# Attention scores on 32-row tiles of the array, causal masks off TensorE, a ring of four PSUM banks

## The reference, cut to what matters

```python
def _L0_attn_ref(x, Wq, bq, Wk, bk, Wv, bv, Wo, bo):
    B, T, C = x.shape
    H, D = (N_HEADS, HEAD_DIM)                # 16 heads of 8
    scale = D ** (-0.5)
    q = (x @ Wq + bq).reshape(B, T, H, D).transpose(0, 2, 1, 3)
    ...
    scores = jnp.einsum('bhqd,bhkd->bhqk', q, k) * scale
    pos = (jnp.arange(T)[:, None] - jnp.arange(T)[None, :]).astype(jnp.float32)
    bias = alibi_slopes(H)[:, None, None] * pos
    scores = scores + bias[None]
    causal = jnp.tril(jnp.ones((T, T), dtype=bool))
    scores = jnp.where(causal, scores, -jnp.inf)
    attn = jax.nn.softmax(scores, axis=-1)
    out = jnp.einsum('bhqk,bhkd->bhqd', attn, v)
    out = out.transpose(0, 2, 1, 3).reshape(B, T, C)
    return out @ Wo + bo
...
x = x + _layernorm(_L0_attn_ref(_layernorm(x, axis=-1), ...), axis=-1)
x = x + _layernorm(_L0_ffn_ref(_layernorm(x, axis=-1), ...), axis=-1)
```

## Time and profile before

| what | us |
|---|---|
| median of 3 runs | 2289.69 (2287.66 to 2295.19) |
| span of the profiled execution | 2287.5 |
| lowest run, beside that span | 2287.66 |

### The profile page before, as it was taken

How to read it: one execution, slowest core, us unless ns; L and a number is a source line. 1 busy time by engine, 2 the same in 40 slices (tenths; PEclk the granted TensorE clock), 3 DMA queues, 4 the chain that set the end, 5 groups by cost and what they waited for, 6 DMA issues and landing times. The chain is left out here.

```text
span 2287.5 us, 41083 instructions
## 1 busy us (share of the span) xinstructions
PE 2102.9 (92%) x11100; PEld 1223.1 (53%) x11100; DVE 1671.8 (73%) x3157; ACT 1373.5 (60%) x2647; POOL 977.3 (43%) x744
## 2 busy tenths in 40 slices
PE   5899999999999679999999999999993999999996
PEld 4455555555554534555555555555531666666664
DVE  5766667666672787777777777778822899998986
ACT  4266566666666616666666666666672655555654
POOL 3665464553610355333333333342002466565554
PEclk7799999999999679999999999999996999999998
DMA  2000000000000300000000000000001100000000
GB/s 59 1 2 1 3 1 1 2 2 1 1 1 2 110 0 1 2 1 1 2 1 1 2 1 1 1 1 1 1 1 61 51 19 19 2 19 19 19 10 10
DMA packets 27508, 24.96 MB, mean 11 GB/s; under 512 B 2409, under 2 KB 21110, under 8 KB 27282
## 3 DMA queue, kind: packets, MB, share of 16 engines
q1 hardware_dynamic: 26400, 21.91, 3.2%
q10 hardware_dynamic: 882, 0.36, 0.1%
HBM read 13.87 MB, written 6.29 MB: 9 GB/s over the span
## 5 line engine op out<-in xcount | busy, mean ns | idle before, releaser
L466 DVE TENSOR_REDUCE at_mx<-at_a 128x1 f32<-128x512 f32 (+3 forms) x1632 | 1010.8, 675 | 358.7 <-PE at_a L333 249.5
L415 ACT ACTIVATE at_probs<-at_b 128x512 f32<-128x512 f32 (+3 forms) x1792 | 888.6, 558 | 474.0 <-PE at_b L360 292.7
L333 PE MATMUL at_a<-at_km,at_fq 128*128 128x512 f32 (+1 forms) x1632 | 704.8, 439 | 20.4 <-DVE at_mx L466 9.8
L360 PE MATMUL at_b<-at_fqm,at_km 128*128 128x512 f32 (+3 forms) x1792 | 710.8, 404 | 11.4 <-ACT at_probs L415 7.6
L333 PEld LDWEIGHTS at_a<-at_km,at_fq 128*128 128x128 f32 x1632 | 316.3, 194 | 290.0 <-DVE at_mx L466 224.4
L360 PEld LDWEIGHTS at_b<-at_fqm,at_km 128*128 128x128 f32 x1792 | 339.8, 191 | 205.5 <-ACT at_probs L415 120.3
L378 PE MATMUL at_pv<-at_probs,at_vst 128*32 128x512 f32 (+3 forms) x3584 | 437.9, 561 | 1.5 <-ACT at_probs L415 1.5
L556 POOL TENSOR_TENSOR at_hi<-at_u,split_sign 128x512 fp32r<-128x512 f32 x120 | 124.9, 1041 | 441.1 <-ACT at_u L404 306.5
L1172 ACT ACTIVATE t_hid<-t_bank_h,b1t 128x512 f32<-128x512 f32 x256 | 174.3, 689 | 195.9 <-DVE t_hid_lo L1306 113.1
L1306 DVE TENSOR_TENSOR t_hid_lo<-t_hid,t_hid_hi 128x512 fp32r<-128x512 f32 x256 | 225.6, 917 | 15.0 <-ACT t_hid_hi L1179 11.8
L569 POOL TENSOR_TENSOR at_km<-at_fk,head_mask 128x2048 fp32r<-128x2048 f32 x60 | 216.1, 3602 | 11.2 <-POOL at_fk L567 11.0
(11 more groups left out here) (211 smaller groups left out, 2410.3 us busy)
## 6 DMA issues: line engine op xcount, KB each, us to landing
t_raw<-L_ffn_W SPq DMA_DIRECT2D x16, 256.0 KB, 3.1
x_first<-L_attn_x SPq DMA_DIRECT2D x4, 512.0 KB, 7.3
second_x_in<-L_attn_x SPq DMA_DIRECT2D x8, 256.0 KB, 3.1
kept<-second_joined SPq DMA_DIRECT2D x8, 256.0 KB, 2.6
kept_u<-second_normed SPq DMA_DIRECT2D x8, 256.0 KB, 2.0
t_heads_in<-tokens SPq DMA_DIRECT2D x8, 256.0 KB, 2.6
t_u_in<-kept_u SPq DMA_DIRECT2D x8, 256.0 KB, 3.1
t_x_in<-kept SPq DMA_DIRECT2D x8, 256.0 KB, 3.1
```

What stands on the lines that cost most here:

```text
L333: mm = pe.matmul(scores, fq[g][:, qt * P:(qt + 1) * P], km[g][:, heads[0]:heads[0] + k, kh * HALF:kh * HALF + w], start=True, stop=not dia ...
L360: mm = pe.matmul(out[:, 0:w], km[g][:, j, kt * P:(kt + 1) * P], fqm[g % 2][:, q0:q0 + w], start=True, stop=not diagonal)
L415: act.activation(probs[(t % 2) * GH + j][:, 0:w], b_bank[n % 3][:, 0:w], ACT.Exp).then_inc(exp_done, 1)
L466: dve.tensor_reduce(mx[:, kh, qt, heads[0]:heads[0] + k], a_bank[n % 3][:, 0:k * w].rearrange("p (k w) -> p k w", k=k), AX.X, ALU.max).the ...
```

## The change

1. Score matmuls contract over 32 partitions, those of their head, for both "a" and "b". The array's other rows stay free for the neighbour in the queue. `km` and `head_mask` go, and with them one instruction of four in the split of keys; `fk` takes the split keys directly.
2. The four "b" of a quad run over the heads 2, 3, 0, 1, so that "a" of head 0, 1, 2, 3 between them lie on other rows.
3. No mask matmuls. An "a" chunk that ends on the diagonal is read by `tensor_tensor_reduce`, which adds a row of zeros and mask and takes the maximum in one pass; chunks are no longer joined over heads (48 in a causal round, 32 of them "ragged", 8 each of 128, 256, 384 and 512 columns; 64 as before in the other attention). For "b" the exponentials of a diagonal quad are taken without a mask and GpSimd's `affine_select` puts zeros over them before "pv", eight quads a round.
4. "a", proj, otr and mtr share one ring of four PSUM banks in the order of the list. "b" keeps three.
5. "b" is three quads ahead instead of two, "pv" trails it by two steps instead of one, and `probs` holds four quads.

```diff
+RING = ("a", "proj", "otr", "mtr")
+A_BANKS = 4
+B_BANKS = 3
+PROBS = 4
...
-                per = max(1, HALF // n)
-                per = 4 if per >= 4 else per
-                for j in range(0, GH, per):
-                    self.chunks.append((qt, kh, list(range(j, j + per)), n))
+                for j in range(GH):
+                    self.chunks.append((qt, kh, j, n))
...
-        self.lead = 2
-        a_steps = nq - 4
+        self.lead = 3
+        a_steps = nq - 2 - self.lead
...
-            dp, p = (ds, q - 1) if q else (0, self.nq - 1)
+            dp, p = (0, i + 1) if i + 1 < self.nq else (1, 0)
...
+def b_head(n):
+    return (n + 2) % GH
...
+                        rows = slice(HW * j, HW * (j + 1))
+                        mm = pe.matmul(misc[:, 0:w], fq[g][rows, qt * P:(qt + 1) * P],
+                                       fk[g][rows, kh * HALF:kh * HALF + w],
+                                       start=True, stop=True)
...
+                        out = b_bank[n % B_BANKS]
+                        rows = slice(HW * j, HW * (j + 1))
+                        mm = pe.matmul(out[:, 0:w], fk[g][rows, kt * P:(kt + 1) * P],
+                                       fqm[g % 2][rows, q0:q0 + w], start=True, stop=True)
...
+                        if n in plan.diagonals:
+                            done(pe, masked, len(plan.diagonals), s, plan.diagonals.index(n))
...
+                        if n in plan.ragged:
+                            ragged = plan.ragged.index(n)
+                            if ragged >= 2:
+                                done(dve, a_read, NA, s, plan.ragged[ragged - 2])
+                            dve.sem_inc(dve_passed, 1)
+                            dve.tensor_tensor_reduce(scrap[ragged % 2][:, 0:w], scores, causal_rows[:, HALF - w:HALF], 1.0,
+                                                     -3.0e38, ALU.add, ALU.max,
+                                                     mx[:, kh, qt, j:j + 1]).then_inc(a_read, 1)
+                        else:
+                            dve.tensor_reduce(mx[:, kh, qt, j:j + 1], scores, AX.X, ALU.max).then_inc(a_read, 1)
...
+                    if what == "b" and n % GH == GH - 1 and n // GH in plan.diagonals:
+                        await_(exp_done, NB, s, n)
+                        block_ = probs[n // GH % PROBS][:, :, 0:P]
+                        pool.affine_select(block_, block_, [[0, GH], [1, P]], ALU.is_ge, 0.0, base=0,
+                                           channel_multiplier=-1).then_inc(masked, 1)
```

More of the change, by code:

```diff
@@ L67, in __init__ @@
                     continue
-                per = max(1, HALF // n)
-                per = 4 if per >= 4 else per
-                for j in range(0, GH, per):
-                    self.chunks.append((qt, kh, list(range(j, j + per)), n))
+                for j in range(GH):
+                    self.chunks.append((qt, kh, j, n))
+        self.ragged = [i for i, (qt, kh, j, n) in enumerate(self.chunks) if causal and kh * HALF + n == (qt + 1) * P]
         self.quads = []
@@ L76, in __init__ @@
                 self.quads.append((qh, kt))
+        self.diagonals = [t for t, (qh, kt) in enumerate(self.quads) if causal and kt * P >= qh * HALF]
         self.na = len(self.chunks)
@@ L135, in body, with places @@
         return out
+    def places(self, steps):
+        order = [step for step in steps if step[0] in RING]
+        return {step: place for place, step in enumerate(order)}
     def prologue(self):
@@ L387, in emit @@
                         mm.then_inc(o_turned, 1)
+                if prologue:
+                    done(pe, proj_read, 4, s0 + 2, 3)
+                    done(pe, fqm_made, 2, s0, 1)
+                    done(pe, a_read, NA, s0 + 1, plan.a_next - 1)
             run(pe, emit)
@@ L458, in emit @@
+                        dve.tensor_tensor(dst[g][:, half], part[:, :], un[:, :], ALU.add).then_inc(split_done, 1)
                     elif what == "a":
-                        qt, kh, heads, w = plan.chunks[n]
+                        qt, kh, j, w = plan.chunks[n]
                         done(dve, a_made, NA, s, n)
                         if n == 0:
-                            if steps[0] == ("proj", 0, 0) and type(b0) is int and ds == 0:
+                            if places is in_prologue and ds == 0:
@@ L547, in emit @@
                         first = False
-                    if type(b0) is int and steps[0] == ("proj", 0, 0) and ds == 0:
+                    if places is in_prologue and ds == 0:
                         continue
```

171 lines of the change are left out of this document (74 added, 97 removed).

## The result

The changed kernel is slower: median 2396.28 us (2366.33 to 2413.76) beside 2288.68 (2285.62 to 2295.19) for the kernel before in the same session, a ratio of 1.042 with a 95% interval of 1.035 to 1.048. The profiled execution of after took 2398.15 us with a span of 2396.4, 109 us over the 2287.5 of before. The forecast was 2067 us, with a range from 1985 up to 2200. The ratios leave out executions that took over 1.5% more than the fastest of the same kernel.

What follows compares the result with a forecast made beforehand. TensorE was taken to bound both attentions now, VectorE after the change. Savings of 152 us in the second attention and 71 us in the first took the 2287.5 us span to 2067 us, range 1985 to 2200.

Steps and rivals of the forecast that it cites:

- The sum: Whole kernel: 15 rounds per attention plus ends, second saves 152 us, first 71 us, giving 2067 us.
- slower, by the clock: Rival, both attentions: granted clock falls to 1.2 GHz, rounds of 73 and 54 us, 2770 us in all; chance 0.03.
- Part 1, row tiles: Score matmuls on 32-row tiles: 0.12 us apart instead of 0.23; VectorE becomes bound, second attention's round 54.1 to 45 us.
- Part 3: Ring and deeper `probs`: no instruction cost, "pv" waits less (0.17 us a step); TensorE's new ring wait within 2 us.
- Part 2, the causal stage: First attention: without masks VectorE becomes the bound at 34.8 us; round 40.65 to 36.5 us, 33 to 39.5.
- dear ragged chunks: Rival, causal attention: new VectorE pass needs two cycles a column, round 52 us, 2299 us in all; chance 0.04.
- dear selects: Rival, causal attention: GpSimd selects set the round from 2.8 us each; at 5.6 us 2405 us; chance 0.02.
- The ends: Prologues and last rounds: 4.6 us saved per prologue, 11 us in the second's last round, 4 in the first's.
- The signs named ahead: Checks in the trace: clock over 0.9, rounds of 36.5 and 45 us; wrong if the first's round grew.

Runs made afterwards that it cites:

- filler4_rows32: The changed kernel plus 448 useless matmuls on 32 rows, one ahead of every fourth "a": 2382.97 us, 1.040 of before.
- before_tiles: The kernel before with score matmuls on the 32 rows of their head, except chunks joined over heads; masks, banks, order kept: 2929.26 us, 1.273 of before.
- pv_early: The changed kernel with each "pv" moved ahead of the last "b" of its step: 2511.57 us, no ratio given.
- filler4: The changed kernel plus 448 useless matmuls on all 128 rows, one ahead of every fourth "a": 2336.91 us, 1.020 of before.
- full_lead2: The changed kernel with scores over 128 rows, zeroed key copies, two quads of `probs`, "b" two ahead, bfloat16 scratch rows: 2290.83 us, 1.0006 of before.
- tiles_lead2: full_lead2 with one thing changed, score matmuls on the 32 rows of their head: 2456.25 us, 1.073 of before.
- mixed2: First attention of before, second of the changed kernel, with full rows for round 0's "a" and the last round's "b": 2253.97 us, 0.983 of before.
- filler_v2: The changed kernel with full-row fillers: every second "a" in causal stage and prologues, every eighth in second attention, last-round quads: 2561.2 us, 1.117 of before.

## Why the prediction was wrong, point by point

**The step that failed: the clock.** The sum had no term for the clock: it put its cost at nothing. The rival "slower, by the clock" came true, and it had 0.03. The same round on tiles takes 36.9 us at 0.96 of the clock and 48.5 at 0.64 (filler4_rows32), and the changed kernel's causal rounds had 0.64 and 48 to 49 us. The prediction argued from the earlier trace rows: 0.98 and 0.92 in a prologue with half as many matmuls. Those matmuls worked on all 128 rows. The row showed that thin full-row work keeps the clock, and it was read as if it spoke of work on a quarter of the rows, of which before has no stretch. It begins at 827 us, too; ahead of it, in the same prologue, the clock was 0.50 (803 to 812 us) and 0.70 (812 to 827). In that same prologue the changed kernel is busy 40.05 of 41 us, more than the 13.14 of 15 of the earlier trace rows, and has 0.50. The right use of the earlier trace rows was to say that no row shows the clock with work on few rows, and to give both levels a chance. The section cited from the Trainium skill ("TensorE: Matmul & The Clock Gate", What's actually happening) has the gate go by how busy TensorE has been. Taken as busy time alone it isn't borne out: 91% busy with 0.64 here, 99% with 0.56 in before_tiles. That it is silent on rows, as the prediction itself noted, was a reason for doubt and not for 0.03. Of the rival's price, 2770 us, only a part came, since the second attention has the full clock in its steady rounds: 0.64 and 0.89 in the windows, and not 0.5 in both.

**Part 1, row tiles.** The overlap is real. After's timeline of TensorE in a steady round, start and us of each (the last rows have the idle time before them and its releaser):

```profile
1347.03 0.50 PE L390 MATMUL at_b<-at_fqm,at_fk 32*128 32x512 f32 x1 [0.53 <-ACT at_probs L449]
...
1348.04 1.06 PE L407 MATMUL at_pv<-at_probs,at_vst 128*32 128x512 f32 x8
...
1349.04 0.49 PE L367 MATMUL at_a<-at_fk,at_fq 32*128 32x512 f32 x1
...
1349.04 0.50 PE L390 MATMUL at_b<-at_fqm,at_fk 32*128 32x512 f32 x1
...
1349.05 0.50 PE L367 MATMUL at_a<-at_fk,at_fq 32*128 32x512 f32 x2
...
1349.38 0.38 PE L390 MATMUL at_b<-at_fqm,at_fk 32*128 32x512 f32 x1
...
1349.38 0.38 PE L367 MATMUL at_a<-at_fk,at_fq 32*128 32x512 f32 x1
...
1349.38 0.39 PE L390 MATMUL at_b<-at_fqm,at_fk 32*128 32x512 f32 x1
...
1350.32 0.50 PE L367 MATMUL at_a<-at_fk,at_fq 32*128 32x512 f32 x1 [0.54 <-DVE at_mx L501]
```

Four scores start within 0.01 us, the next three 0.34 us later: 0.34/4, some 0.085 us each, below both the 0.12 taken and the lower end of 0.105 (it went by the load of a full 128x128 tile; loads of 32 rows are busy 15.84 us for 290 in the steady round, 0.055 us each, where before has 29.21 us for 284, 0.103 each, from 1034 to 1088 us). The estimate by the Trainium skill ("TensorE: Matmul & The Clock Gate", Measured speedup vs the span model), 0.075 us, came nearer. VectorE's own work was sized right: 43.21 us busy in the 51 us round, forecast 43.0. But the round is 50.8 and not 45 us, so its waits were mis-sized: 7.6 us and not 2. The waits of after in that round:

```profile
PEld at_b L390 <- ACT at_probs L449: 14.2, 16, 1.1
PEld at_a L367 <- DVE at_mx L501: 13.5, 17, 1.0
...
DVE at_mx L501 <- PE at_a L367: 6.2, 12, 0.8
```

Sixteen times, once a step, a "b" waits for an exponential: three banks for four "b", so that the fourth needs the first exponential of its own step. Behind it stands "pv" (the row at 1347.03, then 1348.04), and only behind that the next "a". The prediction had VectorE's four banks bridge "pv" alone, 1.7 us; the stop is the fourth "b", a change of tiling, "pv", and a change back. Part 3 named a new wait at the ring of "a" and did not look at the ring of "b", which kept three banks while its matmuls became so fast that they now arrive before ScalarE. pv_early shows that moving "pv" alone doesn't mend it. A fourth bank for "b" wasn't tried.

**Part 2, the causal stage.** The groups of VectorE in after, 60 to 850 us (count, busy us, mean ns, idle before):

```profile
L497 DVE CUSTOM_DVE_ANT_0 at_scrap<-at_a,causal_rows 128x512 f32<-128x512 f32 x128 | 81.2, 686 | 4.0 <-PE at_a L367 4.0
...
L497 DVE CUSTOM_DVE_ANT_0 at_scrap<-at_a,causal_rows 128x128 f32<-128x128 f32 x128 | 36.2, 291 | 38.4 <-PE at_a L367 31.8 <-DVE at_mx L497 1.4
...
L497 DVE DVE_READ_ACCUMULATOR2_ANT at_mx<- 128x1 f32 x512 | 42.6, 83 | 0.0
```

0.686 and 0.291 us against the 0.68 and 0.31 taken from `fqm` and the reductions, and 0.083 us for the second instruction against 0.15: both right or on the cheap side, so the rival "dear ragged chunks" is out. The select has this group on after's page:

```profile
L580 POOL TENSOR_SCALAR_AFFINE_SELECT at_probs<-at_probs 128x512 f32<-128x512 f32 x128 | 81.2, 634 | 350.5 <-ACT at_probs L449 350.3
```

0.634 us, half of the 1.3 taken and below the lower end of 1.0: "dear selects" is out too as a matter of its size. The round forecast, 36.5 us, comes only where the clock is full: 36.9 us in the one such round of filler4_rows32, 38 to 40 us in filler4, with the fillers' own cost in both. That it comes so near is in part luck. VectorE was to need 34.8 us and be the bound, with 1.7 us of waiting; it is busy 28.3 us there and idle 8.5, while TensorE is busy 33.2, fillers included, where 28.3 was forecast. The two errors go against each other. In after, at 0.64 of the clock, TensorE is busy 44.6 of 48.2 us in a round.

**Part 3 and 4.** The deeper `probs` took away the wait for the selects which full_lead2 shows with two quads; in after "pv" waits only 1.0 us for selects in the whole run, by its page. No run separates it further: tiles_lead2 has two quads and is 60 us slower than after, but it makes the key copies too. The ends were to give 24 us (two times 4.6, 11 and 4). In after they lose: the last round of the second attention, from its staging to the last transposes, takes 104.3 us at a clock of 0.75, where before has 91.8 at 1.00, and the start of that attention stands at 0.50. mixed2, with full rows and 1.00 there, has 85.3 us for the last round, 6.5 less than before; 11 were forecast.

**The signs named ahead** did their work. A clock over 0.9 was to show the forecast, and it was 0.803; the first attention's round was not to grow, and it went from 40.65 to about 49 us.

## What to carry to other kernels

Count full-row work and not only instructions or busy time when matmuls are put on row tiles: here they overlapped nearly threefold, and TensorE was granted 0.64 instead of 0.97 of its clock where little else ran on all rows. By these runs row tiles paid only in the second attention, where a "pv" of full width stands in each step (54.1 to 50.8 us a round); try them stage by stage and read the clock of each. Put the last round on full rows (mixed2), and queue all tiles of one shape together, since two changes of tiling cost 0.27 us at the lower clock. When an operation becomes several times faster, look at every ring that it fills, and at what is queued behind the first one that is full.

## What the runs showed of the hardware

- TensorE's mean granted clock depends on the rows in use. Same schedule, 128 or 32 rows for the scores: 0.938 and 0.785 in the mean, 0.91 and 0.60 in the causal attention, with TensorE busy 90% and 87%. Useless matmuls, 192 in the stage, lift the causal clock from 0.64 to 0.84 on 128 rows and to 0.67 on 32.
- Busy is not enough: 99% busy with 0.56 in before_tiles.
- One and the same causal round can fall at either level: 36.9 us at 0.96 and 48.5 at 0.64 in filler4_rows32, 43.2 at 1.00 and 60.5 at 0.66 in filler_v2. What tips it is open.
- Four score matmuls on four row tiles start within 0.01 us, 0.34 us a group at full clock, where full rows take 0.23 us each.
- Changes of tiling cost: a score on 32 rows with its mask on 128 takes 0.94 us at the lower clock, the pair on full rows 0.67, so two changes cost some 0.27 us.
- A select on GpSimd over 512 elements takes 0.634 us; VectorE's sum-and-maximum over 512 columns, one operand in PSUM, 0.686 us, and its read of the result 0.083 us.
- Why the second attention holds the full clock on tiles and the causal one doesn't is only argued: a step there has as many scores, but a "pv" of full width in each of 16 quads, where a causal round has 12 quads with narrower ones at the diagonal. No run isolates it.
